# Moving the residual sums of two layers to TensorE and one layer norm to ScalarE, in a two-layer decoder with a woven instruction order

## The reference

```python
x = _layernorm(x + _L0_attn_ref(x, ...))            # causal self-attention with rotary positions, 16 heads
x = _layernorm(x + _L0_xattn_ref(x, ctx_1024, ...)) # cross attention with per-head norms
x = _layernorm(x + _L0_ffn_ref(x, ...))             # feed-forward, operands rounded to FP4 by blocks of 16
x = _layernorm(x + _L1_attn_ref(x, ...))            # linear attention block with convolutions and a GELU MLP
x = _layernorm(x + _L1_xattn_ref(ctx_1024, x, ...)) # causal attention of the context over x
x = _layernorm(x + _L1_ffn_ref(x, ...))             # 8 experts, the best two of each token
def _layernorm(x, axis=-1, eps=1e-05):
    m = jnp.mean(x, axis=axis, keepdims=True)
    v = jnp.var(x, axis=axis, keepdims=True)
    return (x - m) / jnp.sqrt(v + eps)
```

## Time and profile before

| | us |
|---|---|
| three runs | 747.34, 747.43, 751.6 (median 747.43) |
| the profiled execution | 747.63 |
| its span from first to last instruction | 745.8 |
| PE, DVE, ACT, POOL busy | 557.3, 532.0, 326.2, 203.9 |

### The profile page before, as it was taken

How to read it: one execution, slowest core, us unless ns; L and a number is a source line. 1 busy time by engine, 2 the same in 40 slices (tenths; PEclk the granted TensorE clock), 3 DMA queues, 4 the chain that set the end, 5 groups by cost and what they waited for, 6 DMA issues and landing times.

```text
span 745.8 us, 13887 instructions
## 1 busy us (share of the span) xinstructions
PE 557.3 (75%) x4864; PEld 389.2 (52%) x4864; DVE 532.0 (71%) x1520; ACT 326.2 (44%) x637; POOL 203.9 (27%) x316
## 2 busy tenths in 40 slices
PE   5697668666488869687885696566888797789954
PEld 3466536434255337454674364354453375687841
DVE  7877777898758667657776678987676676765734
ACT  1653345322275556115633462222864551354631
POOL 4304300201100620274024011021016112774533
PEclk9997669888789989769977697976999795699987
DMA  9993100000000000020000000000000000332324
GB/s 293 324 296 108 29 0 2 1 1 0 2 0 1 1 1 2 1 80 14 2 2 0 1 2 1 0 2 0 1 1 0 1 3 1 89 115 71 84 88 115
DMA packets 45555, 32.34 MB, mean 43 GB/s; under 512 B 4280, under 2 KB 43456, under 8 KB 45360
## 3 DMA queue, kind: packets, MB, share of 16 engines
q1 hardware_dynamic: 43216, 26.54, 12.8%
q0 software_dynamic: 2272, 4.92, 1.9%
HBM read 13.83 MB, written 17.62 MB: 42 GB/s over the span
## 4 chain that ended last, share of the span: by engine, by line
PE 46%; DVE 33%; ACT 9%; issue 6%; POOL 2%; DMA 2%; DVEq 0%; SPq 0%; POOLq 0%; ACTq 0%
PE ps L624 5%; PE ps L605 5%; PE ps L668 5%; PE ps L943 5%; PE ps L957 2%; DVE s_row_max L1344 2%; DVE s_probs L1349 2%; ACT s_probs L1084 2%; PE ps L874 2%; PE ps L869 2%; DVE s_r L1313 2%; PE ps L636 2%; DVE s_work L1303 1%; DVE s_work L1300 1%; DVE s_work L1290 1%
## 5 line engine op out<-in xcount | busy, mean ns | idle before, releaser
L1883 POOL TENSOR_TENSOR s_rs<-s_mv,eps 128x1 f32<-128x1 f32 x80 | 16.4, 207 | 347.0 <-DVE s_mv L1319 346.9
L1344 DVE TENSOR_REDUCE s_row_max<-ps 128x16 f32<-128x1024 f32 x48 | 58.7, 1222 | 41.6 <-PE ps L624 41.4
L605 PE MATMUL ps<-tabs,s_probs 128*128 128x128 f32 x384 | 63.2, 295 | 17.1 <-ACT s_probs L1084 15.8
L1064 ACT ACTIVATE s_pT<-ps 128x512 f32<-128x512 f32 x96 | 55.6, 594 | 39.0 <-PE ps L605 38.5
L624 PE MATMUL ps<-s_k,s_q 64*64 64x256 f32 x768 | 61.0, 442 | 9.9 <-ACT s_q L1034 9.9
L605 PEld LDWEIGHTS ps<-tabs,s_probs 128*128 128x128 f32 x384 | 44.2, 148 | 37.7 <-ACT s_probs L1084 25.7
L1084 ACT ACTIVATE s_probs<-s_probs 128x1024 f32<-128x1024 f32 x48 | 50.6, 1056 | 24.5 <-DVE s_probs L1349 24.5
L1349 DVE TENSOR_TENSOR s_probs<-ps,s_row_max 128x1024 f32<-128x1024 f32 x48 | 58.7, 1222 | 1.3
L668 PE MATMUL ps<-s_v,s_pT 128*64 128x18 f32 x1536 | 56.2, 218 | 4.1 <-ACT s_headsT L1075 1.9
L668 PEld LDWEIGHTS ps<-s_v,s_pT 128*64 128x64 f32 x1536 | 52.4, 146 | 11.8 <-issue 11.0
L943 PE MATMUL ps<-s_pT,s_k 128*128 128x128 f32 x312 | 44.5, 287 | 4.6 <-issue 2.8
(11 more groups left out here) (285 smaller groups left out, 1262.9 us busy)
## 6 DMA issues: line engine op xcount, KB each, us to landing
rows_io<-zero_rows SPq DMA_DIRECT2D x9, 1152.0 KB, 11.9
s_probs<-rows_io SPq DMA_DIRECT2D x39, 72.0 KB, 1.9
s_cin<-in_ctx SPq DMA_DIRECT2D x4, 256.0 KB, 3.7
s_xin<-in_x SPq DMA_DIRECT2D x4, 256.0 KB, 4.3
wgu<-in_wg SPq DMA_DIRECT2D x1, 1024.0 KB
wgu<-in_wu SPq DMA_DIRECT2D x1, 1024.0 KB
wo<-in_wo SPq DMA_DIRECT2D x1, 1024.0 KB
s_probs<-shares_io SPq DMA_DIRECT2D x4, 256.0 KB, 5.2
```

Of the source, the lines that this page charges most:

```text
L605: ins = pe.transpose(h.ps[:, 2, tile(j)], h.probs[:, t % 2, 8 * part + 2 * j:8 * part + 2 * j + 2, :] .rearrange("p h k -> p (h k)"), ident)
L1064: act.activation(h.pT[:, t % 2, 4 * part:4 * part + 4, :].rearrange("p j q -> p (j q)"), h.ps[:, 2, :], ACT.Copy).then_inc(h.pT_here.sem, 1)
L1344: dve.tensor_reduce(h.row_max[:, t % 2, :], s3, AX, ALU.max).then_inc(h.max_here.sem, 1)
```

## The change

- Feed-forward: PE's projection group starts with one more matmul, the identity times `h.x[:, t, :]`, so the PSUM region holds the sum. DVE's sum goes; `bn_stats` reads PSUM. The norm moves from DVE to ACT, as scale and bias: POOL makes the bias as -mean (one more instruction) times rstd (another, in a step of its own). The PSUM region is now held until ACT has normed the tile, so PE's projection waits for `x_new` of tile t - 1.
- Linear block: the four transposes of `h.y1` become four pairs of accumulating fp32 matmuls, identity times `h.x` and `h.y1` times identity. DVE's four sums go; `bn_stats` and `norm_x` read PSUM.
- The counts in `EACH` and the waits on `summed`, `eps_added` and `rstd_here` follow.
- All four order tables are new. The number of steps of a stream and of the experts: PE 251, 251, 126 before and after; ACT 191 to 199 for each stream; DVE 572 to 548 (first) and 588 to 564 (second); POOL 115 to 123. Added up along the way, PE's new table has the second stream at most 3 steps away from where the old one has it, for any step of the first. In the last tiles of the feed-forward part of the first pass, PE's old order is, for the first stream, projection of tile 2, transposes of tile 3, projection of tile 3, one after the other; in the new one two steps of the second stream stand ahead of the projection of tile 3.

```diff
+SUMS = {0: 0, 1: 1, 4: 2}
...
                         if u - 3 >= 1:
-                            pe.wait_ge(*h.summed.at(sub * TILES + u - 3))
+                            pe.wait_ge(*h.summed.at(SUMS[sub] * TILES + u - 3))
...
                         if t >= 1:
-                            pe.wait_ge(*h.summed.at(2 * TILES + t))
+                            pe.wait_ge(*h.x_new.at(2 * TILES + t))
+                        pe.matmul(h.ps[:, 3, 0:P], ident, h.x[:, t, :], start=True, stop=False)
                         for k in range(KC):
-                            ins = pe.matmul(h.ps[:, 3, 0:P], h.hT[:, t % 2, tile(k)], d_w[:, k, :], start=k == 0, stop=k == KC - 1)
+                            ins = pe.matmul(h.ps[:, 3, 0:P], h.hT[:, t % 2, tile(k)], d_w[:, k, :], start=False, stop=k == KC - 1)
...
                 for t in range(TILES):
-                    ins = pe.transpose(h.ps[:, 1, tile(t)], h.y1[:, tile(t)], ident)
+                    pe.matmul(h.ps[:, 1, tile(t)], ident, h.x[:, t, :], start=True, stop=False)
+                    ins = pe.matmul(h.ps[:, 1, tile(t)], h.y1[:, tile(t)], ident, start=False, stop=True)
                 ins.then_inc(h.projected.sem, TILES)
...
-                for u in range(TILES + 3):
+                for u in range(TILES + 2):
...
+                    if 0 <= u - 2:
+                        t = u - 2
+                        yield
+                        act.wait_ge(*h.rstd_here.at(2 * TILES + t + 1 + (t + 1)))
+                        act.activation(h.x[:, t, :], h.ps[:, 3, 0:P], ACT.Identity, scale=h.rs[:, t % 2:t % 2 + 1],
+                                       bias=h.mv[:, t % 2, 0:1]).then_inc(h.x_new.sem, 1)
...
-                dve.tensor_tensor(h.r[:, t % 2, :], y, res, ALU.add).then_inc(h.summed.sem, 1)
-                yield
-                dve.wait_ge(*h.summed.at(n))
-                dve.bn_stats(h.st[:, t % 2, :], h.r[:, t % 2, :]).then_inc(h.stat.sem, 1)
+                if res is None:
+                    dve.bn_stats(h.st[:, t % 2, :], y).then_inc(h.stat.sem, 1)
+                else:
...
-                        yield from sum_norm(h, 2, u - 2, h.ps[:, 3, 0:P], h.x[:, u - 2, :])
-                    if 0 <= u - 3:
-                        yield from norm_x(h, 2, u - 3)
+                        yield from sum_norm(h, 2, u - 2, h.ps[:, 3, 0:P], None)
...
-                        yield from sum_norm(h, 3, u, h.ps[:, 1, tile(u)], h.x[:, u, :])
+                        yield from sum_norm(h, 3, u, h.ps[:, 1, tile(u)], None)
                     if u >= 1:
-                        yield from norm_x(h, 3, u - 1)
+                        yield from norm_x(h, 3, u - 1, h.ps[:, 1, tile(u - 1)])
...
                 pool.tensor_tensor(h.rs[:, t % 2:t % 2 + 1], h.mv[:, t % 2, 1:2], eps[:, 0:1], ALU.add).then_inc(h.eps_added.sem, 1)
+                if sub == 2:
+                    pool.tensor_scalar(h.mv[:, t % 2, 0:1], h.mv[:, t % 2, 0:1], -1.0, None, ALU.mult).then_inc(h.eps_added.sem, 1)
...
                                    ALU.pow).then_inc(h.rstd_here.sem, 1)
+                if sub == 2:
+
+                    yield
+                    pool.wait_ge(*h.rstd_here.at(n + t))
+                    pool.tensor_tensor(h.mv[:, t % 2, 0:1], h.mv[:, t % 2, 0:1], h.rs[:, t % 2:t % 2 + 1], ALU.mult).then_inc(h.rstd_here.sem, 1)
```

More of the change, by code:

```diff
@@ L116 @@
 EACH = {"block_act": 18, "block_dve": 26, "block_pe": 21, "block_pool": 4, "c_here": 16, "ct_here": 1, "ct_turned": 1,
-        "den_here": 12, "eps_added": 20, "exped": 12, "ffn_x": 2, "fq": 48, "gated": 4, "hT_here": 4, "headsT_here":
+        "den_here": 12, "eps_added": 24, "exped": 12, "ffn_x": 2, "fq": 48, "gated": 4, "hT_here": 4, "headsT_here":
         12, "heads_here": 12, "heads_turned": 12, "hidden": 4, "hln": 38, "hq_here": 4, "hq_turned": 4, "k4_here": 3,
@@ L120 @@
         "p_turned": 24, "projected": 20, "q4_here": 3, "q_here": 3, "q_proj": 3, "qk_turned": 2, "resid_here": 2,
-        "route_act": 2, "route_dve": 5, "route_pe": 4, "rstd_here": 20, "rt": 24, "scores": 12, "sent": 128,
-        "shifted": 12, "silu_here": 4, "squared": 2, "stat": 20, "stored": 16, "summed": 20, "v2_here": 3, "v_proj":
+        "route_act": 2, "route_dve": 5, "route_pe": 4, "rstd_here": 24, "rt": 24, "scores": 12, "sent": 128,
+        "shifted": 12, "silu_here": 4, "squared": 2, "stat": 20, "stored": 16, "summed": 12, "v2_here": 3, "v_proj":
         3, "x_here": 16, "x_new": 20, "xt_here": 6, "xt_turned": 6}
@@ L1312, in sum_norm @@
                     dve.wait_ge(*h.x_new.at(n - 2))
-                dve.tensor_tensor(h.r[:, t % 2, :], y, res, ALU.add).then_inc(h.summed.sem, 1)
-                yield
-                dve.wait_ge(*h.summed.at(n))
-                dve.bn_stats(h.st[:, t % 2, :], h.r[:, t % 2, :]).then_inc(h.stat.sem, 1)
+                if res is None:
+                    dve.bn_stats(h.st[:, t % 2, :], y).then_inc(h.stat.sem, 1)
+                else:
+                    dve.tensor_tensor(h.r[:, t % 2, :], y, res, ALU.add).then_inc(h.summed.sem, 1)
+                    yield
+                    dve.wait_ge(*h.summed.at(SUMS[sub] * TILES + t + 1))
+                    dve.bn_stats(h.st[:, t % 2, :], h.r[:, t % 2, :]).then_inc(h.stat.sem, 1)
                 yield
@@ L1322, in norm_x @@
                 yield
-                dve.wait_ge(*h.rstd_here.at(sub * TILES + t + 1))
+                dve.wait_ge(*h.rstd_here.at(sub * TILES + t + 1 + (TILES if sub > 2 else 0)))
                 dst = h.pay[:, t, 0:P] if sub == 4 else h.x[:, t, :]
@@ L1883, in rstd @@
                 pool.tensor_tensor(h.rs[:, t % 2:t % 2 + 1], h.mv[:, t % 2, 1:2], eps[:, 0:1], ALU.add).then_inc(h.eps_added.sem, 1)
+                if sub == 2:
+                    pool.tensor_scalar(h.mv[:, t % 2, 0:1], h.mv[:, t % 2, 0:1], -1.0, None, ALU.mult).then_inc(h.eps_added.sem, 1)
                 yield
-                pool.wait_ge(*h.eps_added.at(n))
+                pool.wait_ge(*h.eps_added.at(n + (t + 1 if sub == 2 else TILES if sub > 2 else 0)))
                 pool.tensor_tensor(h.rs[:, t % 2:t % 2 + 1], h.rs[:, t % 2:t % 2 + 1], minus_half[:, 0:1],
                                    ALU.pow).then_inc(h.rstd_here.sem, 1)
+                if sub == 2:
+                    yield
+                    pool.wait_ge(*h.rstd_here.at(n + t))
+                    pool.tensor_tensor(h.mv[:, t % 2, 0:1], h.mv[:, t % 2, 0:1], h.rs[:, t % 2:t % 2 + 1], ALU.mult).then_inc(h.rstd_here.sem, 1)
             def block_rstd(h, n):
```

## The result

The changed kernel takes 763.3 us (median of four runs), the kernel before 749.5 in the same comparison (its three runs and one more): a ratio of 1.018, 95% interval 1.012 to 1.024. The forecast was 746.2, with 752 as its upper end. It was wrong: about 14 us in place of -1.4. On another chip, where the kernel before takes 770.8 us, the changed kernel gave 1.019 (1.015 to 1.023), so the loss isn't a matter of the chip.

The account below looks back on a forecast made before the run. No engine alone was taken to bound it: DVE leads in the feed-forward stretches, PE at the linear block's end. Feed-forward -4.6, linear block +3.2 and order 0 gave -1.4 us against 747.6, so 746.2; range 739.5 to 752.

Parts of the forecast that it names:

- New order: All four order tables: same steps in nearly the same interleaving, so 0, from -3 to +3 us for all.
- Feed-forward, DVE: Feed-forward stretches, where DVE leads: six sums and five norms taken off DVE save 3.3 us a pass, ends 0 and 5.2.
- The held PSUM region: Feed-forward: the next tile's projection waits for ACT's norm where two tiles come close; 0.4 us a pass, ends 0 and 3.0.
- The end of the norm: Last feed-forward tile before the linear block: POOL's two further instructions and ACT's longer norm add 0.6 us a pass, bounds 0.1 and 1.2.
- End of the linear block: Eight matmuls replace four transposes, four DVE sums go: +1.34 first stream, +0.3 second; 1.6 us a pass, ends 0 and 2.7.
- the price of the matmuls: Rival, linear block's ends: eight matmuls at four times a transpose's rate take 3.5 us, +6.8 in all, 753.0; chance 0.03.
- the hold: Rival, feed-forward: projections wait for ACT at close pairs in both streams, 3.0 us a pass, 751.4 in all; chance 0.12.

Follow-up runs that it names:

- two splices: Kernel before with the new order only up to the end of the first cross attentions: 1.007; changed kernel with the old order up to there: 1.0085.

## Why the prediction was wrong

*"New order ... 0, from -3 to +3 us"* is the step that failed most. The new tables by themselves cost 13.8 us with the old operations. I judged them by how far a stream is displaced in PE's (at most three steps), which says nothing of what stands in front of what on the other three queues. What they do instead shows in two places. In the feed-forward part they lengthen f by 5.7 and 4.6 us; the place and the amount are shown, the wait that does it is not. In the first stretch they cost 0.7 to 1.0 per cent in time, as two splices show, and +7.1 us in the profile. There the loss follows TensorE's granted clock, 0.83 against 0.87, and what in the order lowers it stays open. POOL's held power at 57 us, the first suspect, made DVE wait 0.68 us.

*"Feed-forward, DVE"*, -3.3 us a pass: DVE's busy time in the first of these stretches fell by 2.9 us (45.3 for 48.2), so the price of the work was about right, but DVE did not lead as assumed. It was 87% busy in the stretch, yet with the order held fixed at the new one, all of the change together shortens f by 1.4 and 0.9 us, and putting eight sums back (with the region freed at the same time) changes it by +1.4 and -0.6. That the time goes round a loop through PE, ACT and POOL instead is what the waits suggest; no run isolates it.

*"The held PSUM region"*, 0.4 us a pass of a possible 3.0: the mechanism was right, the latency too (2.6 us for 2.4), its size was not. Within the old order it is 5.1 and 1.9 us a pass, above my upper end in one of them. The rest may be ACT's waiting for POOL. I let the norms "fit in at no cost" on an ACT with 43 us of idle time, but idle time isn't free for an instruction that must wait in a queue: it stood there 12.7 us in the changed kernel and 19 to 38 in the old order. Forecast for the part -2.3 us a pass, measured +4.3 and +3.7. A second PSUM region for the projection, the direct remedy, was not tried, though the projection takes only 128 of the 512 columns of its bank.

*"The end of the norm"*, +0.6: before, 1.48 us passed from the last mean's start to the norm's end; now 208.63 to 210.69, 2.06: +0.58.

*"End of the linear block"*, +1.6 a pass and +3.2 in all: 0.45% (3.4 us) for both passes alone, with an interval from 1.7 to 5.0 us; in the profile of the changed kernel +1.2 and +1.7. This term held. The price of its matmuls shows in the chain in order of time, second pass, to be read beside the earlier trace rows:

```profile
591.35 0.49 PE ps L891 x2
591.84 0.22 PE ps L892 x2
592.06 0.22 PE ps L891 x2
592.28 0.22 PE ps L892 x2
...
593.44 0.31 DVE s_st L1324
```

And the last norm of the same four tiles, from DVE's timeline:

```profile
597.69 0.41 DVE L1338 TENSOR_SCALAR s_x<-ps,s_mv,s_rs 128x128 f32<-128x128 f32 x1 [0.43 <-POOL s_rs L1899]
```

Eight matmuls from 591.35 to 593.41 are 2.1 us, of which 0.27 is the first one's start, at 0.22 us each as priced. Behind them DVE needs 4.25 us from its first statistics to the start of its last norm, for 5.23 before and 4.1 in the forecast. The Trainium skill (TensorE: Matmul & The Clock Gate, section Terms) calls the transpose mode four times faster for fp32; these rows, beside the 0.11 us of a transpose in the earlier trace rows, show two times, so the rival that rested on it is out.

*The range.* It ended at 752 because beside the price of the matmuls the only mechanism on the slow side was the hold. That two kernels with the same instructions can differ by 1.6% through their order alone was left out of the range altogether.

## What to carry to other kernels

Where the order of in-order queues is written out, treat a new order as a part of the change with a price of its own, of the size of a per cent, and measure it with the old operations too. A wait in front of a step that could run is worth looking for, but price it by who waits for that step: here 7.46 us of POOL's idle time cost DVE 0.68 us. When two profiles differ, find the first instruction that is late and compare it with the first one that the edit touches; if it comes earlier, the edit isn't the cause of what was lost so far. A busy share of 87% didn't make an engine the one whose work can be taken off at full price. Count the turns from engine to engine before a buffer comes free, and remember that a waiting instruction on an idle engine blocks that engine. And a schedule made for one set of operations is a bad measure of another: compare each in the order made for it.

## What the runs showed of the hardware

TensorE's granted clock differs between kernels of the same instructions in another order, and also between profiles of kernels that are the same up to the place. The changed kernel, profiled on two chips, fell to 0.50 at the same two places (31 and 55 us), while two kernels that differ from it only in POOL's order, from 56 us on, kept 1.00 at both. With the same instructions the first 65 us then took 4.8 us longer. The feed-forward stretch doesn't follow it so: 58.6 to 58.8 us in the first pass of six profiles with the changed operations in the new order, at a mean granted clock from 0.67 to 0.73. The two chips' profiles of one kernel agree within 0.1 us in it. What differs is mostly the end: 121 to 125 us on the chips with 749 us for the kernel before, 138 to 145 on those with 771 to 774.
